# Masks, denominators and state of the Taylor attention put in another order on VectorE, and TensorE four score units behind instead of five

## The chip, the cores and the metric

One core of one Trainium2 chip runs the whole program. The metric is the time of one execution on the device in microseconds (us). The engines are TensorE (PE, with its weight loads PEld), VectorE (DVE), ScalarE (ACT), GpSimd (POOL) and SyncE (SP), which issues the DMAs. All five run their own instruction streams in order and meet at semaphores.

## The reference, cut to what matters

The input is 8 sequences of 1024 tokens of width 256. Each is layer-normed, and the output is the input plus two branches: a linear attention with a Taylor feature map (16 heads of width 16), which the change touches, and a two-layer transformer with local attention, which it does not.

```
xn = layernorm(x)                                     # (8, 1024, 256)
q, k, v = heads of xn @ Wq.T, xn @ Wk.T, xn @ Wv.T    # 16 heads of width 16
f(u)  = [1, u / 2, u_i * u_i / (4 * sqrt(2)), u_i * u_j / 4 for i < j]
y_t   = sum over s <= t of (f(q_t) . f(k_s)) * v_s  /  sum over s <= t of (f(q_t) . f(k_s))
out   = x + y @ Wo.T + transformer(xn)
```

The kernel uses that f(q) . f(k) is, up to a factor, (q.k + 4)^2 + 16. So a tile of scores is a matmul, a square with bias 4 on ACT, and a sum with 16; on a diagonal tile DVE also multiplies by the causal mask.

## The kernel before

The program does the Taylor attention for the 8 sequences first (0 to about 930 us), then the transformer. Within the first part, `project` and `attention` alternate: `project(b + 1, b)` makes q, k and v of the next sequence and finishes the output of the last one.

`attention(b)` goes over four groups of four heads, and each group over 14 score units (`UNITS`). Units 0 to 9 are the near tiles: five steps of two units each (a unit holds two heads). Unit 10 is the state: the first four key tiles, taken as 160 quadratic forms (`psi`, written by POOL's `pairs` and DVE's `other_rows`) times the values (`state`, L774). Units 11 and 12 are the forms applied to the late queries (L811), unit 13 the remaining forms (`rest`, L804).

- PE computes the scores of unit n (L816, L811, L804) into a ring of three bank pairs, so it first waits until unit n - 3 has been consumed. BEHIND units later it runs `attend` (L832, L839, L842), which multiplies the values with the squared and masked weights. With BEHIND = 5, `attend` of step 2 stands behind unit 10 and that of step 3 behind unit 12. After unit 11 stands `turn_state` (L782, L784), which transposes the state.
- ACT squares each unit (L663, L658 for unit 13) into `weights`. There are three sets of them, so the first unit of a step waits for `attend` of three steps before.
- DVE masks the diagonal tiles of each step (`mask_diagonals`, L452), copies the state out of PSUM (`keep_state`, L459), copies it back turned (`turn_state`, L466 and L467), adds the sums of earlier tiles to the result (`add_before`, L443, one for each half of the tokens), and prepares psi for the next group (`other_rows`, L480 to L490).
- The denominators of groups 0 to 2 go a longer way. After both L443 of a group, SP copies the denominator rows into a flat tile (L221), DVE inverts them (`invert_den`, L388), SP copies them back (L225), DVE spreads them over the partitions (`spread_den`, L393 and L395), and POOL multiplies (L320; after group 1 it also adds group 0, L323). Group 3 is normalised by DVE in eight pieces (`normalise`, L406 to L413), which wait for POOL's third L320.
- DVE also does other work in the groups: statistics of the next sequence (L367 in group 0, L372 and L375 in group 1), its layer norm (L382, four tiles in each of groups 2 and 3) and, in groups 1 and 3 of sequences 5 and 6, a scaling of tables (L537).
- SP's queue in a sequence is: `load_heads` of group 2 (12 DMAs, L254, once group 0's scores are all done), `invert` of group 0 (L221, then L225 once DVE has inverted), `load_heads` of group 3 (once group 1's scores are done), `invert` of group 1, `invert` of group 2, then the stores and loads for the next sequence.

In the names below, `shared` holds psi and the state, `t_ps` is PSUM, `qkT` are the transposed heads and `vals` the values.

Of the kernel before, what the change touches and what calls it, by code (L numbers as in the profile page):

```python
# [15 lines left out]
ALU = mybir.AluOpType  # L16
# [10 lines left out]
TH, TD = 16, 16  # L27
GROUPS, GH = 4, 4
# [9 lines left out]
ROW_PAIRS, ROW_SQUARES, ROW_LINEAR, ROW_ONE = 0, len(PAIRS_IJ), len(PAIRS_IJ) + TD, len(PAIRS_IJ) + 2 * TD  # L38
# [23 lines left out]
def taylor_block(nc, B, x, wqk, wv, wo, ident, causal, earlier, eps_rows, keep_rows, forms, own_head, later, xn_d, attn_d, parts_d, xnT_d,  # L62
                 id_s, ao, rot, qks_s, last_stored):

    with ExitStack() as ctx:
# [36 lines left out]
        psi = space[:, 0:PAST * GH * FORMS].rearrange("p (th f) -> p th f", f=FORMS)  # L102
# [93 lines left out]
        def unit_bank(n):  # L196
            return 2 + 2 * (n % RING)
# [163 lines left out]
        def _(dve):  # L361
            v = nc.vector

            def tile_stats(b, t):
                if t == 0:
                    dve.wait_ge(x_in, 16 * b + 16)
                v.bn_stats(st[:, t, :], xs[:, t, :]).then_inc(stats, 1)  # L367
# [9 lines left out]
            def layer_norm(b, t):  # L377
                if t == 0:
                    dve.wait_ge(rstd_ready, b + 1)
                    if b >= 1:  # L380
                        dve.wait_ge(stored, 16 * (2 * b - 1))
                v.tensor_scalar(xn[:, t, :], xs[:, t, :], mv[:, t, 0:1], rstd[:, t:t + 1],  # L382
                                ALU.subtract, ALU.mult).then_inc(xn_ready, 1)

            def invert_den(b, g):

                dve.wait_ge(den_in, 16 * (b * (GROUPS - 1) + g + 1))
                v.reciprocal(den_flat[:, :], den_flat[:, :]).then_inc(den_inverse, 1)  # L388

            def spread_den(b, g):  # L390

                dve.wait_ge(den_out, 16 * (b * (GROUPS - 1) + g + 1))
                v.stream_shuffle(den[:, :], den[:, :], [ONE[g % 2]] * 32).then_inc(spread, 1)  # L393
                dve.wait_ge(spread, 2 * (b * (GROUPS - 1) + g) + 1)
                v.tensor_scalar_mul(den[:, :], den[:, :], keep_s[:, g % 2:g % 2 + 1]).then_inc(spread, 1)  # L395
# [40 lines left out]
            def attention(b, following):  # L436
                def add_before(g, half):

                    tiles = slice(half * TILES // 2, (half + 1) * TILES // 2)
                    if g == 0 and half == 0:  # L440
                        dve.wait_ge(before_ready, b + 1)
                    dve.wait_ge(pv_done, (b * GROUPS + g) * AS + LAST_STEP[half] + 1)
                    v.tensor_tensor(yT[:, g, half * 512:(half + 1) * 512].rearrange("p (t n) -> p t n", n=P),  # L443
                                    ps[:, half, :].rearrange("p (t n) -> p t n", n=P),
                                    before[:, g, tiles].unsqueeze(2).to_broadcast([P, TILES // 2, P]), ALU.add).then_inc(yT_ready, 1)

                def mask_diagonals(g, i):
                    w = GH * ((g * AS + i) % RING)
                    dve.wait_ge(squared, (b * GROUPS + g) * SQUARES + 2 * i + 2)
                    for o, width in DIAGONALS[i]:  # L450
                        a = weights[:, w:w + GH, o:o + width]
                        last = v.scalar_tensor_tensor(a, a, 16.0, causal_s[:, 0:width].unsqueeze(1).to_broadcast([P, GH, width]),  # L452
                                                      ALU.add, ALU.mult)
                    last.then_inc(diag, 1)

                def keep_state(g):
                    group = b * GROUPS + g
                    dve.wait_ge(state_ps, group + 1)
                    v.tensor_copy(state_T, ps[:, unit_bank(g * NU + 2 * NS), 0:FORMS]).then_inc(state_kept, 1)  # L459

                def turn_state(g):
                    group, bank = b * GROUPS + g, unit_bank(g * NU + 2 * NS) + 1
                    dve.wait_ge(turned_ps, group + 1)
                    if group:
                        dve.wait_ge(pv_done, group * AS)
                    v.tensor_copy(state_main, ps[:, bank, 0:P])  # L466
                    v.tensor_tensor(state_rest, ps[:, bank, P:2 * P], own_s[:, 0:P], ALU.mult).then_inc(state_ready, 1)  # L467

                def other_rows(g):

                    group = b * GROUPS + g
                    if g == 0:
                        dve.wait_ge(krows_ready, PAST * (b + 1))
                        for half in parts_out:
                            dve.wait_ge(half, 16 * (BLOCKS // 2) * (b + 1))
                    if group:
                        dve.wait_ge(state_ps, group)
                    k = krows[:, g].rearrange("p t h d -> p (t h) d")
                    squares = psi[:, :, ROW_SQUARES:ROW_SQUARES + TD]
                    v.tensor_tensor(psi[:, :, ROW_LINEAR:ROW_LINEAR + TD], k, k, ALU.max)  # L480
                    v.reduce_sum(ksum[:, :], k, AX).then_inc(ksum_ready, 1)
                    dve.wait_ge(ksum_ready, 4 * group + 1)
                    v.tensor_scalar_add(ksum[:, :], ksum[:, :], 1.0).then_inc(ksum_ready, 1)
                    dve.wait_ge(ksum_ready, 4 * group + 2)
                    v.scalar_tensor_tensor(squares, k, 2.0, ksum[:, :].unsqueeze(2).to_broadcast([P, PAST * GH, TD]), ALU.mult, ALU.subtract)\
                        .then_inc(ksum_ready, 1)
                    v.tensor_scalar(psi[:, :, ROW_ONE:FORMS], ksum[:, :].unsqueeze(2).to_broadcast([P, PAST * GH, FORMS - ROW_ONE]),
                                    -1.0 / (FORMS - ROW_ONE), 3.0 / (FORMS - ROW_ONE), ALU.mult, ALU.add).then_inc(ksum_ready, 1)
                    dve.wait_ge(ksum_ready, 4 * group + 4)
                    v.tensor_tensor(squares, squares, k, ALU.mult).then_inc(psi_rest, 1)  # L490

                for g in range(GROUPS):
                    mask_diagonals(g, 0)
                    if g >= 1:
                        add_before(g - 1, 1)
                    if following is not None and g == 0:
                        for t in range(4):
                            tile_stats(following, t)
                    mask_diagonals(g, 1)
                    if g == 0:  # L500
                        other_rows(0)
                    if g >= 2:
                        spread_den(b, g - 2)
                    if following is not None:
                        if g == 0:
                            for t in range(4, TILES):
                                tile_stats(following, t)
                        if g == 1:
                            variances(following)
                        if g % 2 and b >= len(later):  # L510
                            scale_tables((b - len(later)) * 2 + g // 2)
                        if g >= 2:
                            for t in range(2):
                                layer_norm(following, (g - 2) * TILES // 2 + t)
                    mask_diagonals(g, 2)
                    if following is not None and g >= 2:
                        for t in range(2, 4):
                            layer_norm(following, (g - 2) * TILES // 2 + t)
                    mask_diagonals(g, 3)
                    keep_state(g)  # L520
                    mask_diagonals(g, 4)
                    turn_state(g)
                    add_before(g, 0)
                    if g + 1 < GROUPS:
                        other_rows(g + 1)
                    if g >= 1:
                        invert_den(b, g - 1)
                add_before(GROUPS - 1, 1)
                spread_den(b, GROUPS - 2)

            def scale_tables(quarter):

# [142 lines left out]
        def _(pe):  # L675
# [81 lines left out]
            def attention(b):  # L757
# [86 lines left out]
                    last.then_inc(pv_done, 1)  # L844

                units = GROUPS * NU
                BEHIND = 5
                last_of = {}
                for n in range(units):
                    kind, i, pair = UNITS[n % NU]  # L850
# [1 line left out]
                ends = {n: step for step, n in last_of.items()}  # L852
                for n in range(units + BEHIND):
                    if n < units:
                        scores(n)
                    if n - BEHIND in ends:
                        attend(*ends[n - BEHIND])
                    if n % NU == 2 * NS + 1 and n < units:
# [956 lines left out]
```

## Time and profile before

| what | us |
|---|---|
| median of three runs | 3529.01 |
| the three runs | 3529.01, 3528.80, 3537.74 |
| the profiled execution | 3529.01 |
| its span | 3527.10 |
| PE busy in the span | 3357.0 (95%) |
| DVE busy | 2763.9 (78%) |
| ACT busy | 2512.4 (71%) |
| POOL busy | 1575.1 (45%) |

The shares of the whole span mix two parts. In the last 2597 us the PE has next to no gap; in the first 930 us every engine has gaps, and the change is in that part only. So the times that matter are read inside one group of one sequence, from the timeline, and the part as a whole from the table of stretches.

### The profile page before, as it was taken

What the parts mean: (1) busy time and instruction counts of PE and PEld (TensorE: products, weight loads), DVE (VectorE), ACT (ScalarE), POOL (GpSimd) and SP (SyncE); (2) the same over time, 40 slices, a digit from 0 to 9 for tenths busy, and PEclk for the clock granted to TensorE, in tenths of its full rate; (3) what the DMA queues carried; (4) which work ended last, traced back from release to release, by engine and by line L of the source; (5) the groups of instructions that cost most, each with busy time, mean ns of one, the idle gap of its engine ahead of it and who ended that gap; (6) DMA issues with size and microseconds to landing.
All of it is one profiled execution on the core that took longest, in us unless ns stands there. A gap on an engine that the chain in (4) does not pass through costs nothing.

```text
span 3527.1 us, 96731 instructions
## 1 busy us (share of the span) xinstructions
PE 3357.0 (95%) x36960; PEld 2506.0 (71%) x36960; DVE 2763.9 (78%) x8288; ACT 2512.4 (71%) x5597; POOL 1575.1 (45%) x1675
## 2 busy tenths in 40 slices
PE   7888888889699999999999999999999999999999
PEld 4544554445378787887878878788787887878877
DVE  4767776776688888878888788887888888888886
ACT  5556665666377777777777777777777777777775
POOL 4445544454344444444444444444444444444443
PEclk9999999999899999999999999999999999999999
DMA  6646765567322222222222222222222222222211
GB/s 158 140 124 116 168 142 117 108 113 145 104 62 67 68 61 72 66 69 68 61 72 66 69 68 61 72 66 68 68 61 72 66 68 68 61 72 66 69 46 42
DMA packets 289965, 293.94 MB, mean 83 GB/s; under 512 B 40960, under 2 KB 221536, under 8 KB 288992
## 3 DMA queue, kind: packets, MB, share of 16 engines
q1 hardware_dynamic: 289504, 287.74, 34.0%
q8 instruction: 295, 4.83, 0.6%
q14 instruction: 166, 1.36, 0.1%
HBM read 104.89 MB, written 58.73 MB: 46 GB/s over the span
## 4 chain that ended last, share of the span: by engine, by line
PE 72%; DVE 1%; POOL 0%; ACT 0%; issue 0%; DMA 0%; SPq 0%; DVEq 0%; POOLq 0%
PE f_ps L1548 18%; PE f_ps L1656 16%; PE f_ps L1668 9%; PE f_ps L1633 6%; PE f_ps L1612 4%; PE f_ps L1553 3%; PE f_ps L1575 3%; PE f_ps L1593 3%; PE f_ps L1622 2%; PE f_ps L1582 2%; PE f_ps L1661 2%; PE f_ps L1597 2%; PE f_ps L1640 1%; PE f_ps L1534 0%; ACT pr L1464 0%
## 5 line engine op out<-in xcount | busy, mean ns | idle before, releaser
L1219 POOL TENSOR_TENSOR turned<-qk,rot 128x256 f32<-128x256 f32 x512 | 406.3, 814 | 1247.4 <-ACT qk L1431 1234.4
L1548 PE MATMUL f_ps<-wqkv_s,hT 128*128 128x512 f32 x1536 | 707.2, 596 | 9.2 <-DMA hT<-xnT_dram 5.7
L1656 PEld LDWEIGHTS f_ps<-hnT,w_s 128*128 128x128 f32 x5120 | 591.7, 192 | 62.9 <-issue 59.7
L1299 DVE CUSTOM_DVE_ANT_0 pr<-f_ps,masks_s 128x192 f32<-128x192 f32 x1024 | 326.5, 355 | 359.5 <-PE f_ps L1582 357.5
L1656 PE MATMUL f_ps<-hnT,w_s 128*128 128x128 f32 x5120 | 592.6, 275 | 2.5 <-DVE hnT L1356 2.5
L1464 ACT ACTIVATE pr<-pr,nmax,rnorm 128x192 f32<-128x192 f32 x1024 | 545.1, 535 | 43.4 <-DVE nmax L1306 43.4
L1548 PEld LDWEIGHTS f_ps<-wqkv_s,hT 128*128 128x128 f32 x1536 | 277.2, 191 | 273.4 <-issue 186.4
L1316 DVE TENSOR_SCALAR pr<-pr,rsum 128x192 f32<-128x192 f32 x1024 | 446.8, 498 | 9.0
L1668 PE MATMUL f_ps<-w_s,act_u 128*128 128x256 f32 x1536 | 352.8, 380 | 0.0
L663 ACT ACTIVATE weights<-t_ps,four_s 128x1024 f32<-128x1024 f32 x320 | 330.4, 1120 | 27.3 <-PE t_ps L842 12.5
L1226 POOL TENSOR_TENSOR rnorm<-ssq,f_mhalf 128x8 f32<-128x8 f32 x128 | 255.8, 1998 | 163.5 <-DVE ssq L1276 163.5
L1668 PEld LDWEIGHTS f_ps<-w_s,act_u 128*128 128x128 f32 x1536 | 282.2, 190 | 32.7
L1453 ACT ACTIVATE kT<-f_ps 128x512 f32<-128x512 f32 x128 | 76.4, 597 | 293.3 <-PE f_ps L1553 293.3
L337 POOL TENSOR_TENSOR shared<-krows 128x240 f32<-128x240 f32 (+14 forms) x480 | 251.5, 559 | 65.2 <-PE t_ps L774 33.2
L1488 ACT ACTIVATE act_u<-f_ps,b_s 128x128 f32<-128x128 f32 x640 | 205.1, 364 | 105.0 <-PE f_ps L1661 89.8
L1633 PE MATMUL f_ps<-fwo_s,oT 128*128 128x256 f32 x1024 | 242.5, 380 | 0.3 <-ACT oT L1477 0.3
L452 DVE SCALAR_TENSOR_TENSOR weights<-weights,causal_s 128x512 f32<-128x512 f32 (+1 forms) x192 | 185.5, 984 | 71.0 <-ACT weights L663 70.8
L832 PE MATMUL t_ps<-weights,vals 128*32 128x512 f32 (+3 forms) x2048 | 191.0, 478 | 38.7 <-DVE weights L452 35.7
L816 PE MATMUL t_ps<-qkT 96*32 96x128 bf16 (+3 forms) x4096 | 188.9, 305 | 31.2 <-ACT weights L663 19.3
L1266 DVE TENSOR_TENSOR cosine<-qk,rot 128x512 f32<-128x512 f32 x256 | 207.7, 811 | 11.8 <-ACT qk L1431 11.8
L1366 DVE SCALAR_TENSOR_TENSOR act_u<-f_ps,b_s,act_u 128x128 f32<-128x128 f32 (+1 forms) x768 | 208.3, 340 | 6.7 <-ACT act_u L1488 4.2
L1233 POOL TENSOR_TENSOR rnorm<-ssq,f_mhalf 128x8 f32<-128x8 f32 x128 | 208.9, 1632 | 0.0
(150 smaller groups left out, 6827.3 us busy)
## 6 DMA issues: line engine op xcount, KB each, us to landing
vw<-vw SPq DMA_DIRECT2D x628, 128.0 KB, 2.4
qkT<-parts_dram SPq DMA_DIRECT2D x384, 128.0 KB, 5.7
kT<-kT SPq DMA_DIRECT2D x124, 256.0 KB, 2.7
parts_dram<-shared SPq DMA_DIRECT2D x64, 384.0 KB, 2.6
xnT_dram<-xnT SPq DMA_DIRECT2D x8, 1025.0 KB, 4.7
xs<-x_dram SPq DMA_DIRECT2D x8, 1024.0 KB, 7.3
xn_dram<-xn SPq DMA_DIRECT2D x8, 1024.0 KB, 5.1
attn_dram<-ao SPq DMA_DIRECT2D x8, 1024.0 KB, 9.9
```

The costliest lines, as they stand in the source:

```text
L337: last = g.tensor_tensor(psi[:, :, o:o + width], k[:, :, i:i + 1].to_broadcast([P, PAST * GH, width]), k[:, :, i + 1:TD], ALU.mult)
L663: a.activation(weights[:, w:w + 2, :], ps[:, bank:bank + 2, :], ACT.Square, bias=four_s[:, :] if kind == "near" else zero_s[:, :]).then_in ...
L1219: g.tensor_tensor(turned[:, heads, f], qk[:, heads, z], sines, ALU.mult).then_inc(done, 1)
L1226: g.tensor_tensor(rnorm[:, HEADS:], ssq[:, HEADS:], mhalf[:, HEADS:], ALU.pow).then_inc(knorm_ready, 1)
L1233: g.tensor_tensor(rnorm[:, :HEADS], ssq[:, :HEADS], mhalf[:, :HEADS], ALU.pow).then_inc(qnorm_ready, 1)
L1299: last = v.tensor_tensor_reduce(out=chances(h), in0=ps[:, SCORES[p], k * 256:k * 256 + BAND], in1=mask_of(it)[:, HALF - k * HALF:HALF - k ...
L1316: last = v.tensor_scalar_mul(chances(h), chances(h), rsum[:, h:h + 1])
L1464: last = a.activation(chances(h), chances(h), ACT.Exp, bias=nmax[:, h:h + 1], scale=rnorm[:, h:h + 1], accum_out=psum[:, h:h + 1])
L1548: last = mm(ps[:, b, :], rows, wqkv_s[:, l, c, i * INNER:(i + 1) * INNER], start=(c == 0), stop=(c == KC - 1))
L1633: last = mm(ps[:, WO, 0:DIM], oT[:, c, :], wo_s[:, l, c, :], start=(c == 0), stop=(c == INNER // P - 1))
L1656: last = mm(ps[:, UP[j // 2], o:o + P], w1_s[:, l, c, half * FULL + j * P:half * FULL + j * P + P], hnT[:, c, :], start=(c == 0), stop=(c ...
L1668: last = mm(ps[:, DOWN, 0:DIM], act_u[:, j, :], w2_s[:, l, j, :], start=(j == 0), stop=(j == FB - 1))
```

## The change

Four edits, all in the Taylor attention:

1. `other_rows` copies k with `tensor_copy` instead of `tensor_tensor(k, k, max)` (L480).
2. DVE's order in a group changes. `add_before(g, 0)` now stands ahead of `keep_state(g)`, and both behind the mask of step 4. `invert_den(g - 1)` moves from the end of the group to behind the mask of step 2.
3. `spread_den(g - 1)` now stands between `keep_state(g)` and `turn_state(g)`; before, it stood one group later, behind the mask of step 1, and for group 2 at the end of the sequence.
4. BEHIND is 4 instead of 5. So `attend` of step 2 stands ahead of the state, and that of step 3 ahead of `turn_state`.

```
-                    v.tensor_tensor(psi[:, :, ROW_LINEAR:ROW_LINEAR + TD], k, k, ALU.max)
+                    v.tensor_copy(psi[:, :, ROW_LINEAR:ROW_LINEAR + TD], k)
...
                     mask_diagonals(g, 1)
                     if g == 0:
                         other_rows(0)
-                    if g >= 2:
-                        spread_den(b, g - 2)
...
                     mask_diagonals(g, 2)
+                    if g >= 1:
+                        invert_den(b, g - 1)
                     if following is not None and g >= 2:
                         for t in range(2, 4):
                             layer_norm(following, (g - 2) * TILES // 2 + t)
                     mask_diagonals(g, 3)
+                    mask_diagonals(g, 4)
+                    add_before(g, 0)
                     keep_state(g)
-                    mask_diagonals(g, 4)
+                    if g >= 1:
+                        spread_den(b, g - 1)
                     turn_state(g)
-                    add_before(g, 0)
                     if g + 1 < GROUPS:
                         other_rows(g + 1)
-                    if g >= 1:
-                        invert_den(b, g - 1)
                 add_before(GROUPS - 1, 1)
-                spread_den(b, GROUPS - 2)
...
-                BEHIND = 5
+                BEHIND = 4
```

On PE, around the state of a group, the row before is this (L774 state, L832 attend, L811 units 11 and 12, L782 and L784 the turn, L804 unit 13):

```order
L774 MATMUL t_ps<-shared,vals 32x160 x16
L832 MATMUL t_ps<-weights,vals 32x384 x4
L832 MATMUL t_ps<-weights,vals 32x128 x4
L811 MATMUL t_ps<-qkT,forms_s 32x512 x8
L782 MATMUL t_ps<-id_s,shared 32x128 x4
L784 MATMUL t_ps<-id_s,shared 32x128 x4
L811 MATMUL t_ps<-qkT,forms_s 32x512 x8
L832 MATMUL t_ps<-weights,vals 32x256 x8
L804 MATMUL t_ps<-qkT,forms_s 32x512 x4
L816 MATMUL t_ps<-qkT 32x512 x8
L832 MATMUL t_ps<-weights,vals 32x384 x4
L832 MATMUL t_ps<-weights,vals 32x128 x4
```

and after the change, where every line number from here on is one lower (L831 is attend, L810 are units 11 and 12, L815 the near scores):

```order
L831 MATMUL t_ps<-weights,vals 32x384 x4
L831 MATMUL t_ps<-weights,vals 32x128 x4
L773 MATMUL t_ps<-shared,vals 32x160 x16
L810 MATMUL t_ps<-qkT,forms_s 32x512 x8
L831 MATMUL t_ps<-weights,vals 32x256 x8
L781 MATMUL t_ps<-id_s,shared 32x128 x4
L783 MATMUL t_ps<-id_s,shared 32x128 x4
L810 MATMUL t_ps<-qkT,forms_s 32x512 x8
L803 MATMUL t_ps<-qkT,forms_s 32x512 x4
L831 MATMUL t_ps<-weights,vals 32x384 x4
L831 MATMUL t_ps<-weights,vals 32x128 x4
L815 MATMUL t_ps<-qkT 32x512 x32
```

Attend of step 2 (the first two rows) has passed the state, attend of step 3 (the 32x256 row) has passed the turn and unit 12, and attend of step 4 has passed the first scores of the next group.

On DVE, group 2 of a sequence from the mask of step 1 on stands like this before (L452 masks, L393 and L395 the spread, L382 layer norm, L459 keep, L466 and L467 turn, L443 add):

```order
L393 STREAM_SHUFFLE den<-den 128x1024
L395 TENSOR_SCALAR den<-den,keep_s 128x1024
L382 TENSOR_SCALAR xn<-xs,t_mv,t_rstd 128x256 x2
L452 SCALAR_TENSOR_TENSOR weights<-weights,causal_s 128x4x256
L382 TENSOR_SCALAR xn<-xs,t_mv,t_rstd 128x256 x2
L452 SCALAR_TENSOR_TENSOR weights<-weights,causal_s 128x4x128 x2
L459 COPY shared<-t_ps 128x160
L452 SCALAR_TENSOR_TENSOR weights<-weights,causal_s 128x4x256
L466 COPY shared<-t_ps 128x128
L467 TENSOR_TENSOR shared<-t_ps,own_s 128x128
L443 TENSOR_TENSOR yT<-t_ps,before 128x512
```

and like this after it:

```order
L382 TENSOR_SCALAR xn<-xs,t_mv,t_rstd 128x256 x2
L452 SCALAR_TENSOR_TENSOR weights<-weights,causal_s 128x4x256
L388 RECIPROCAL den_flat<-den_flat 128x32
L382 TENSOR_SCALAR xn<-xs,t_mv,t_rstd 128x256 x2
L452 SCALAR_TENSOR_TENSOR weights<-weights,causal_s 128x4x128 x2
L452 SCALAR_TENSOR_TENSOR weights<-weights,causal_s 128x4x256
L443 TENSOR_TENSOR yT<-t_ps,before 128x512
L459 COPY shared<-t_ps 128x160
L393 STREAM_SHUFFLE den<-den 128x1024
L395 TENSOR_SCALAR den<-den,keep_s 128x1024
L466 COPY shared<-t_ps 128x128
```

The copy of the state (L459) has gone behind the last mask and behind L443, which waits for attend of step 3; the reciprocal stands ahead of the mask of step 3; the spread stands inside the turn.

## Rows read from the trace of the kernel before

**Rows 1.** Stretches: busy time of each engine, clock share, DMA share, GB/s.

```profile
0.00:930.00 930.00, 781.70 (x9952) 441.43 (x9952) 653.54 (x1248) 576.41 (x866) 429.91 (x632) 0.94 0.59 127
930.00:3527.00 2597.00, 2575.31 (x27008) 2064.53 (x27008) 2110.35 (x7040) 1935.99 (x4731) 1145.22 (x1044) 1.00 0.26 68
```

**Rows 2.** Timeline, sequence 3, group 0: start, us, engine, line, idle before and releaser.

```profile
391.62 10.15 ACT L663 ACTIVATE weights<-t_ps,four_s 128x1024 f32<-128x1024 f32 x10 [0.18 <-PE t_ps L816]
...
400.52 2.79 DVE L452 SCALAR_TENSOR_TENSOR weights<-weights,causal_s 128x1024 f32<-128x1024 f32 x3
...
401.87 1.07 PE L832 MATMUL t_ps<-weights,vals 128*32 128x384 f32 x16
...
402.73 0.64 PE L811 MATMUL t_ps<-qkT,forms_s 96*32 96x512 bf16 x8
...
403.24 0.31 DVE L459 COPY shared<-t_ps 128x160 f32<-128x160 f32 x1
...
404.73 1.11 ACT L663 ACTIVATE weights<-t_ps,zero_s 128x1024 f32<-128x1024 f32 x1 [0.20 <-PE t_ps L811]
...
405.69 0.69 DVE L443 TENSOR_TENSOR yT<-t_ps,before 128x512 f32<-128x512 f32 x1 [0.47 <-PE t_ps L832]
```

**Rows 3.** Timeline, sequence 3, group 1, SP, ACT and PE.

```profile
405.80 6.63 SPq L254 DMA_DIRECT2D qkT<-parts_dram  x12
...
406.40 1.11 ACT L663 ACTIVATE weights<-t_ps,four_s 128x1024 f32<-128x1024 f32 x1
...
415.52 1.29 PE L774 MATMUL t_ps<-shared,vals 128*32 128x160 f32 x32
416.63 1.05 PE L832 MATMUL t_ps<-weights,vals 128*32 128x384 f32 x16
```

**Rows 4.** Timeline, sequence 3, group 2.

```profile
420.74 4.24 ACT L663 ACTIVATE weights<-t_ps,four_s 128x1024 f32<-128x1024 f32 x4
...
424.17 6.96 SPq L254 DMA_DIRECT2D qkT<-parts_dram  x12
...
426.64 1.34 DVE L393 STREAM_SHUFFLE den<-den 128x1024 f32<-128x1024 f32 x1
...
428.69 2.78 DVE L382 TENSOR_SCALAR xn<-xs,t_mv,t_rstd 128x256 f32<-128x256 f32 x2
428.85 2.47 POOL L320 TENSOR_TENSOR yT<-yT,den 128x1024 f32<-128x1024 f32 x1 [4.31 <-DVE den L395]
...
431.17 0.56 SPq L221 DMA_DIRECT2D den_flat<-yT  x1
...
432.92 1.21 DVE L382 TENSOR_SCALAR xn<-xs,t_mv,t_rstd 128x256 f32<-128x256 f32 x2
...
434.04 1.90 DVE L452 SCALAR_TENSOR_TENSOR weights<-weights,causal_s 128x512 f32<-128x512 f32 x2
...
440.59 1.11 ACT L663 ACTIVATE weights<-t_ps,four_s 128x1024 f32<-128x1024 f32 x1
```

**Rows 5.** DMA packets from 435 to 437 us (den_flat's are the 128-byte ones).

```profile
DMA packets 215, 0.15 MB, mean 77 GB/s; under 512 B 155, under 2 KB 155, under 8 KB 214
```

**Rows 6.** Timeline, end of sequence 3: last attend, next sequence's transposes, DVE's chain.

```profile
462.10 1.04 PE L842 MATMUL t_ps<-shared 128*32 128x512 f32 x8
...
463.07 0.66 PE L685 MATMUL t_ps<-id_s,xn 128*128 128x128 f32 x4
...
475.00 0.69 DVE L419 TENSOR_TENSOR rest<-t_ps,shared 128x512 f32<-128x512 f32 x1 [0.68 <-ACT shared L595]
```

**Rows 7.** Timeline, end of sequence 7, the last.

```profile
905.73 0.69 DVE L443 TENSOR_TENSOR yT<-t_ps,before 128x512 f32<-128x512 f32 x1 [2.79 <-PE t_ps L842]
...
911.32 0.30 DVE L406 STREAM_SHUFFLE den<-yT 128x128 f32<-128x128 f32 x1 [0.36 <-issue]
```

**Rows 8.** Groups of instructions by line, DVE, first 930 us.

```profile
L480 DVE TENSOR_TENSOR shared<-krows 128x256 f32<-128x256 f32 x32 | 17.9, 559 | 0.0
```

**Rows 9.** Stretch 457 to 460 us, columns as in rows 1.

```profile
457.00:460.00 3.00, 3.00 (x40) 1.60 (x36) 1.25 (x3) 1.11 (x1) 0.00 (x0) 0.51 0.00 0
```

## The prediction

> **What bounds the kernel now.** I first read the table of stretches [rows 1]. In the last 2597 us PE is busy 2575 of them and the change does not reach it; all that can move lies in the first 930 us, where PE is busy 782, DVE 654, ACT 576 and POOL 430. No engine is full there, so waits inside a group decide, and the next view is the timeline of one group. I take sequence 3 and count from a group's first square on ACT. The reader should see that ACT's ten near squares run without a gap in group 0 (10.15 us for ten, one each 1.0 us, [rows 2]), and that every gap comes after them, where ACT waits for units 11 and 12. Groups 0 and 1 last 14.8 (391.62 to 406.40) and 14.3 us (406.40 to 420.74); groups 2 and 3 have the layer norm and the spread on DVE, and group 2 lasts 19.85 (420.74 to 440.59) [rows 2 to 4]. From group 3's first square to PE's first transpose of the next sequence it is 463.07 - 440.59 = 22.5 us [rows 4, 6]. From there on PE, ACT and DVE go hand in hand to the next sequence. DVE is not the late one: its first subtraction there (L419) still waits 0.68 us for ACT [rows 6].
>
> **Group 0: what the new order costs.** Before, `keep_state` (L459) ran at 403.24, as soon as the mask of step 3 was done, and unit 12 was squared at 404.73, that is 13.1 us into the group [rows 2]. In the change L459 stands behind the mask of step 4 and behind L443, and L443 waits for attend of step 3, which itself has the state and unit 11 ahead of it on PE. Step by step, from the group's start: the mask of step 2 begins at 8.9 (the three L452 begin at 400.52), attend of step 2 can start at 10.2, as now (401.87). Before, the state was already done by then; now it comes behind. Attend takes 0.86 (401.87 to 402.73 on PE), the state 1.11 (415.52 to 416.63 [rows 3]), unit 11 0.44 (an estimate from the 0.64 of its row less the overlap): attend of step 3 starts at 12.65. L443 can read 1.2 later, 13.85 (its wait ends 405.69, with attend of 16 matmuls begun just before), takes 0.69, and L459 0.31: 14.8. PE's turn takes 0.44 and unit 12 ends 0.66 after its start, so its square begins at 15.9 instead of 13.1. Square 13 follows at 16.9. The next group's first score now stands behind attend of step 4 as well: rest scores at 16.05, attend 16.25 to 17.1, the score 0.6, so the next group starts at 17.75. Group 0: **+3.0 us**. The masks and squares themselves hide nothing of it, because ACT has nothing else to square: all three rings are full.
>
> **Group 1.** Here there is a gain first: attend of step 5 stands one unit earlier, so ACT's fifth square starts at 4.0 instead of 4.8. The mask of step 2 can be done at 7.4 (square 5 done at 6.1, the mask 1.2). Then DVE reaches the moved reciprocal (L388), and this adds a wait: it needs the denominators, which SP fetches (L221) only behind the 12 DMAs of `load_heads`. Their first is issued when the last group's scores are done, 0.6 before the group's start now (405.80) and, by the steps above, 1.3 before it then. In group 2 the 12 go out from 424.17, L221 at 431.17, and 155 of its packets under 512 bytes (it has 128; a few tiny ones are others) are only seen from 435 to 437 [rows 4, 5]: about 12.3 us from the first of the 12 to the last byte. With that distance the reciprocal runs at 11.0 - 0.3 = 10.7 in group 1, which I take; the bounds are 7.4 (no wait at all, if the small DMA came at its own pace) and 12. Queued behind it on DVE are the masks of steps 3 and 4, and PE's attend of step 3 waits for the first of them. Masks of step 3 beside POOL's pairs take 1.90 (434.04 [rows 4]): done 12.9; attend of step 3; mask of step 4 to 14.1; L443 to 14.75; L459 15.05; then the spread (L393 and L395, from 426.64 to 428.69, 2.05) to 17.1, beside which PE's turn and unit 12 are hidden; turn on DVE 0.5 to 17.6; rest scores, attend, first score, 0.2 + 0.86 + 0.66: 19.4 against 14.3, **+5.1 us**. Without the wait it would be 17.1, +2.8.
>
> **Group 2.** The spread and POOL's multiply are gone from ahead of the mask of step 2. That was worth 2.05, and 1.57 more, since the first pair of L382 took 2.78 beside POOL's L320 and the second 1.21 [rows 4]. So the mask of step 2 is done at 7.5 instead of 12.2. But the reciprocal again waits, to 10.9 (12.3 from 1.4 before the start). Then: reciprocal 0.34, L382 pair 1.2, masks 1.9, mask 1.2, L443 and L459 1.0, spread 2.05, turn 0.5, and 1.7 for PE as before: 20.6 against 19.85, **+0.7 us**. Without the wait 18.4, -1.4.
>
> **Group 3 and the end.** No loads stand ahead of L221 here, so no wait. POOL's L320 and L323 now run around the group's start and hold the first two masks to about 6.2. From there: L382 pair, mask, reciprocal, pair, masks, mask come to 12.6, L443 and L459 to 13.6, spread 15.7, turn 16.2, rest scores 16.5, the two last attends 0.86 and 1.8 to 19.2. That is 22.5 - 19.2 = **-3.3 us**. In sequences 0 to 6 nothing more comes of DVE's freed 2.05 and of the POOL multiply at the end (DVE waits for ACT there). Only in sequence 7 do they sit in the open: from the end of the last L443 (906.42) to the first L406 (911.32) are 4.9 us [rows 7], of which some 4.5 go, with a group 3 shorter by some 3: -7. Its group 2 has no layer norm in either kernel, so it gains less: +2.
>
> **The clock.** PE's granted clock was 0.51 from 457 to 460 us [rows 9], its 1.2 GHz level, after PE had stood waiting for L459. It now waits so, 1 to 2.5 us at a time, in all four groups, not in two. What stands in the open behind the wait is rest scores, attend, first score: 1.7 us at 2.4 GHz, so up to 1.7 more per group, nothing at the least. I take 0.5 each, nearer to nothing since groups 0 and 1 run with shorter gaps: +2.0 per sequence.
>
> **Copy for max (L480).** 559 ns each, 32 times, 17.9 us in all [rows 8]. DVE then waits for squares 0 and 1 of the next group anyway, and that hides it: nothing. The bounds are -0.3 and +2.5 us each in the group's wait, the latter if it is caught behind an L320.
>
> **Two rules of the Trainium skill.** In the trace the denominators' packets came after the twelve loads' [rows 4, 5]. The Trainium skill, DMA: Bandwidth & Descriptors, section Queues, rings and completion order, says that on each DMA engine descriptors of a ring are consumed in ring order, and that engines alternate only between rows; L221 and the loads are both SP's. By that rule the wait on L388 is sure; the trace agrees, and the sum above has it.
> L382 beside L320 took 2.78 for a pair instead of 1.21. The Trainium skill, SBUF — State Buffer, section Who interferes with whom, says that DVE and GpSimd share a port pair as a lock held for the whole instruction, and names copies and instructions with two SBUF inputs among those that take it. By that rule the loser waits for up to a whole L320, and the new L480 is no safer than the old one; the price of it is the third rival.
>
> **Sum.** Sequences 0 to 6: 3.0 + 5.1 + 0.7 - 3.3 + 2.0 = +7.5 each, 52.5 together. Sequence 7: 3.0 + 5.1 + 2 - 7 + 2 = +5, of which I take 3, as its gaps are uneven. Together +55.5. On the profiled execution's 3529.01 (span 3527.10 and 1.9 around it), which is also the median, that gives **3584 us**.
>
> **Rivals.**
> 1. The denominators land in time. For it: in group 1 the loads need not be as slow as in group 2, whose 12.3 I measured. Against: both move the same amount. Groups 1 and 2 then come to +2.8 and -1.4, a sequence to +3.1 with the clock and +1.1 without: 3529 + 22 + 1 = 3552, or 3536 without the clock's part.
> 2. Faster: DVE's own work is the path in groups 2 and 3, so the 3.6 us (2.05 + 1.57) taken from ahead of the mask of step 2 arrive whole in both, and the chain L443, L459, turn hides beside it. It decides if the denominators are there by 7.4 us and if the two groups give back more than the 3.0 + 2.8 that groups 0 and 1 lose: -7.2 + 5.8 = -1.4, seven times, and -7 at the end: 3512. Against it: L459 has four things more ahead of it than before.
> 3. POOL's multiplies fall on the masks of groups 2 and 3 whole: 2.5 each (L320 took 2.47), of which I have some 0.4 in group 2 and part in group 3. About +4 a sequence: 3529 + 55 + 28 = 3612. Against: they start while DVE does `other_rows`.
> 4. The half clock in all four groups whole: 4 x 1.7 - 2.0 = 4.8 more each: about 3620.
>
> **How the numbers follow.** A difference within 0.3% (10.6 us) is one that a measurement cannot tell from none. The forecast has 0.60, rival 1 0.15, rival 2 0.10, rivals 3 and 4 together 0.15. Faster: rival 2 but for its nearest part, and a little for unseen gains, 0.10. Same: the low half of rival 1, 0.07. Slower 0.83. The range runs from the low part of rival 1, 3541, to 3608, short of rivals 3 and 4; the forecast's own is 3565 to 3600.
>
> **What would show it.** In the changed profile: PE's wait for L459 in all four groups and ACT's wait for units 11 and 12 (L810 there) well above before; a DVE wait of 2 to 4 us for a DMA at the reciprocal in groups 1 and 2, and none in group 3; groups 0 and 1 at 17 to 20 us; L382 pairs of 1.2 us; group 3 shorter; nothing changed after the Taylor part. If the reciprocal does not wait, group 1 is near 17 and rival 1 holds. If groups 0 and 1 stay under 16, the chain through L443 is wrong, and with it the sign.

## The result, and the profile after

The changed kernel takes 3592.11 us (median of four runs, 3582.77 to 3600.04) against 3532.41 for the kernel before (four runs): a ratio of 1.0167, 95% interval [1.0131, 1.0203]. A second comparison of almost the same kernel (the change with the old max, below) gave 1.0168 [1.0154, 1.0182]. The forecast was 3584. The profiled execution took 3588.62, its span is 3586.8.

The table of stretches, cut where the Taylor part ends, answers to [rows 1]: stretch, busy time of PE, PEld, DVE, ACT and POOL, clock share, DMA share, GB/s.

```profile
0.00:987.00 987.00, 802.98 (x9952) 441.29 (x9952) 629.84 (x1248) 575.09 (x866) 397.49 (x631) 0.92 0.56 119
987.00:3586.00 2599.00, 2578.08 (x27008) 2064.50 (x27008) 2110.58 (x7040) 1936.11 (x4731) 1145.54 (x1045) 1.00 0.26 68
```

The second part is as long as before (2599 to 2597 us). The first is 57 us longer. ACT and DVE do no more work in it than before, and PE is busy for 21 us more with the same matmuls, at a lower mean clock share: most of the 57 us is waiting. The waits of the first part name where (who waited for whom, us, times, longest). First the kernel before, in its 930 us:

```profile
ACT weights L663 <- PE t_ps L811: 114.4, 53, 7.6
PE t_ps L832 <- DVE weights L452: 35.7, 15, 5.4
```

and the changed kernel, in its 987 us:

```profile
ACT weights L662 <- PE t_ps L810: 164.4, 52, 8.1
PE t_ps L831 <- DVE weights L452: 60.8, 23, 4.3
DVE den_flat L388 <- DMA den_flat<-yT: 57.7, 16, 4.9
```

Two waits have grown, and the last line has no counterpart before: the reciprocal waits 16 times, 3.6 us each on average, in groups 1 and 2 of the eight sequences. Sequence 3 shows both costs. First group 0, which answers to [rows 2] (start, us, engine, line, idle before and its releaser):

```profile
409.02 10.15 ACT L662 ACTIVATE weights<-t_ps,four_s 128x1024 f32<-128x1024 f32 x10 [0.18 <-PE t_ps L815]
...
419.08 1.07 PE L831 MATMUL t_ps<-weights,vals 128*32 128x384 f32 x16 [2.24 <-DVE weights L452]
419.94 1.98 PE L773 MATMUL t_ps<-shared,vals 128*32 128x160 f32 x32
...
424.34 0.69 DVE L443 TENSOR_TENSOR yT<-t_ps,before 128x512 f32<-128x512 f32 x1 [3.07 <-PE t_ps L831]
424.94 0.32 DVE L459 COPY shared<-t_ps 128x160 f32<-128x160 f32 x1
425.31 0.43 PE L781 MATMUL t_ps<-id_s,shared 128*32 128x128 f32 x8 [1.10 <-DVE shared L459]
...
426.44 1.11 ACT L662 ACTIVATE weights<-t_ps,zero_s 128x1024 f32<-128x1024 f32 x1 [2.51 <-PE t_ps L810]
```

The near squares still run without a gap, and attend of step 2 starts 10.1 us into the group, as forecast (10.2). Then come the state, unit 11, attend of step 3, L443 and L459 one behind the other: L459 starts 15.9 us into the group (11.6 before) and unit 12's square 17.4 us (13.1 before). Each is about 1.5 us later than the working had them (about 14.5, and 15.9). The state took 1.98 us, not 1.29 as in [rows 3]: PE had waited 2.24 us, and from 419 to 424 us its granted clock was 0.66, so it was at the lower level (1.2 GHz) for most of that time.

Group 1, against [rows 3]:

```profile
428.32 10.15 ACT L662 ACTIVATE weights<-t_ps,four_s 128x1024 f32<-128x1024 f32 x10 [0.20 <-PE t_ps L815]
...
433.42 0.57 SPq L221 DMA_DIRECT2D den_flat<-yT  x1
...
440.63 0.35 DVE L388 RECIPROCAL den_flat<-den_flat 128x32 f32<-128x32 f32 x1 [4.92 <-DMA den_flat<-yT]
440.90 3.05 DVE L452 SCALAR_TENSOR_TENSOR weights<-weights,causal_s 128x512 f32<-128x512 f32 x3
...
442.73 1.94 PE L831 MATMUL t_ps<-weights,vals 128*32 128x256 f32 x16 [4.18 <-DVE weights L452]
...
447.68 1.11 ACT L662 ACTIVATE weights<-t_ps,zero_s 128x1024 f32<-128x1024 f32 x1 [7.96 <-PE t_ps L810]
447.77 2.35 POOL L320 TENSOR_TENSOR yT<-yT,den 128x1024 f32<-128x1024 f32 x1 [2.12 <-DVE den L395]
...
448.00 2.27 DVE L480 COPY shared<-krows 128x256 f32<-128x256 f32 x1
```

The reader should follow one wait through three engines: DVE stands 4.92 us for the denominators, so the mask of step 3 is late, PE stands 4.18 us for it with attend of step 3, and ACT stands 7.96 us ahead of unit 12. The wait also costs PE its clock. The stretches of group 1, in the kernel before and in the changed one (columns as above), have a clock share of 1.00 and 0.78:

```profile
406.40:420.70 14.30, 13.73 (x284) 7.88 (x280) 10.81 (x27) 12.92 (x14) 9.19 (x17) 1.00 0.65 129
428.00:451.00 23.00, 16.93 (x284) 7.98 (x276) 13.85 (x29) 13.20 (x14) 11.40 (x17) 0.78 0.54 82
```

Group 2 repeats the wait, 2.78 us long. There the pair of L382 no longer meets L320 [rows 4]:

```profile
456.12 0.73 DVE L382 TENSOR_SCALAR xn<-xs,t_mv,t_rstd 128x256 f32<-128x256 f32 x2
...
461.51 0.35 DVE L388 RECIPROCAL den_flat<-den_flat 128x32 f32<-128x32 f32 x1 [2.78 <-DMA den_flat<-yT]
...
473.46 4.12 ACT L662 ACTIVATE weights<-t_ps,four_s 128x1024 f32<-128x1024 f32 x4 [1.87 <-PE t_ps L815]
```

Sequence 3 is not a mean one: it lost 12.6 us, the most of all; the others lost 2.8 to 8.2. Taken from ACT's squares in sequences 0 to 6, the mean time from a group's first square to the next group's is (group 3's includes the projection behind it):

| us | group 0 | group 1 | group 2 | group 3 | sum |
|---|---|---|---|---|---|
| before | 15.2 | 15.4 | 19.8 | 61.9 | 112.3 |
| after | 18.4 | 22.2 | 21.7 | 57.5 | 119.9 |
| difference | +3.2 | +6.8 | +1.9 | -4.4 | +7.6 |
| forecast, with 0.5 for the clock | +3.5 | +5.6 | +1.2 | -2.8 | +7.5 |

### The profile page after: what moved, and what is told of

Its sections match the earlier page's. It is cut to its first block, busy times and chain, and to the rows that moved or that the text cites. A ratio compares the mean times of both kernels' runs of the same rounds, so it can differ in the third digit from the quotient of the medians.

```text
span 3586.8 us, 96731 instructions
## 1 busy us (share of the span) xinstructions
PE 3381.1 (94%) x36960; PEld 2505.8 (70%) x36960; DVE 2740.4 (76%) x8288; ACT 2511.2 (70%) x5597; POOL 1543.0 (43%) x1675
## 4 chain that ended last, share of the span: by engine, by line
PE 71%; DVE 1%; ACT 0%; issue 0%; POOL 0%; DMA 0%; SPq 0%; DVEq 0%; POOLq 0%
PE f_ps L1547 18%; PE f_ps L1655 16%; PE f_ps L1667 9%; PE f_ps L1632 6%; PE f_ps L1611 4%; PE f_ps L1552 3%; PE f_ps L1574 3%; PE f_ps L1592 3%; PE f_ps L1621 2%; PE f_ps L1581 2%; PE f_ps L1660 2%; PE f_ps L1596 2%; PE f_ps L1639 1%; PE f_ps L1533 0%; ACT pr L1463 0%; DVE pr L1298 0%
## 5 line engine op out<-in xcount | busy, mean ns | idle before, releaser
L337 POOL TENSOR_TENSOR shared<-krows 128x240 f32<-128x240 f32 (+14 forms) x480 | 227.4, 510 | 187.8 <-PE t_ps L773 157.0
L452 DVE SCALAR_TENSOR_TENSOR weights<-weights,causal_s 128x512 f32<-128x512 f32 (+1 forms) x192 | 176.8, 946 | 105.0 <-ACT weights L662 104.8
L831 PE MATMUL t_ps<-weights,vals 128*32 128x512 f32 (+3 forms) x2048 | 193.2, 490 | 64.6 <-DVE weights L452 60.8
L1282 DVE TENSOR_TENSOR qk<-cosine,turned 128x512 f32<-128x512 f32 x256 | 206.8, 808 | 0.0
```

The costliest lines, as they stand in the source:

```text
L337: last = g.tensor_tensor(psi[:, :, o:o + width], k[:, :, i:i + 1].to_broadcast([P, PAST * GH, width]), k[:, :, i + 1:TD], ALU.mult)
```

## The experiments

All ratios are to the kernel before. Each experiment's group times are means as in the table above.

**BEHIND alone.** The kernel before with

```
-                BEHIND = 5
+                BEHIND = 4
```

> The kernel before with BEHIND = 4 alone; DVE's order, the denominators and the max as before. Theory: TensorE's order is only part of the cost. In group 0 attend of steps 2 and 3 now stand ahead of the state and the turn, unit 12's square comes at about 14.6 instead of 13.1, the group lasts 16.5 to 17 us (15.2 before, 18.4 in the change); group 1 about 14.5, groups 2 and 3 within 1 us of before. In all +15 to +25 us over the kernel before (about 3550). Rival: BEHIND alone is the cost: +45 us or more, group 0 at 18 us. Second rival: one unit less behind frees ACT's rings sooner and nothing else happens: -5 to -15 us.

Measured: 3525.6 us, 0.9976 [0.9965, 0.9986]. My theory had the direction in group 0 right and its size too small (17.7, +2.6, where I had 16.5 to 17), and it had the sum wrong: 10 us less instead of 15 to 25 more. Groups 2 and 3 gave back 1.8 and 1.6 us. The number is that of the second rival, but not its mechanism, since group 0 does lose. In groups 2 and 3 the masks are late: in sequence 3, group 2 of the kernel before, PE stood 1.59 us for L459 with attend of step 3 still behind the turn; here that attend runs ahead of the turn, and PE does not stand there. So this part of the change, by itself, is a small gain and not a part of the loss.

**The copy alone**, the first edit of the change.

> The kernel before with the tensor_copy of L480 alone. Theory: the copy takes less than the 559 ns of the max, but DVE waits for squares right after it: no change (within 3 us). Rival: the copy is held by whole GpSimd instructions and delays masks: +5 us or more, with single copies of 1 us and longer.

Measured: 3535.9, 1.0004 [0.9990, 1.0018]. No change.

**The keep back in its place**, in the changed kernel:

```
                     mask_diagonals(g, 3)
+                    keep_state(g)
                     mask_diagonals(g, 4)
                     add_before(g, 0)
-                    keep_state(g)
```

> The changed kernel with keep_state back ahead of the mask of step 4 (add_before(g, 0) stays ahead of spread and turn). Theory: the chain L443, L459, turn is what group 0 loses, so group 0 goes from 18.4 to about 16.5 us; in groups 1 to 3 unit 12 is squared 2 to 3 us sooner, but VectorE's turn still stands behind L443 and the spread and ends the group, so these change by less than 1 us. In all -15 to -25 us against the changed kernel (about 3570). Rival: the late keep costs in every group: -50 us or more. Second rival: keep's place is indifferent: within 5 us.

Measured: 3568.0, 1.0100 [1.0078, 1.0123], 24 us below the change. Group 0 went from 18.4 to 17.35, with unit 12 squared at 14.6 us instead of 15.9 (medians of sequences 0 to 6), and groups 1 to 3 changed by 0.7 us or less. The sum is as expected. Group 0, which I had at 16.5, is not, and in groups 1 to 3 unit 12's square came only 0.8 to 1.5 us sooner (means), where I had 2 to 3.

**The denominators' DMA from ScalarE**, in the changed kernel; L221 leaves SP's `invert`:

```
+                    if n % NU == 6 and n > NU:
+                        ...
+                        act.dma_start(den_flat[:, :], yT[ONE[g % 2]:P:VP, g, :]).then_inc(den_in, 16)
                     act.wait_ge(score_ps, b * GROUPS * SQUARES + squares_to(n) + 1)
```

> The changed kernel with the first denominator DMA (L221) issued by ScalarE ahead of its square of unit 6 instead of by SyncE behind the 12 loads. Theory: the reciprocal's wait comes from the place in SyncE's queue, so the DMA lands some 2 to 3 us after its issue, the reciprocal runs at about 8 to 9.5 us in groups 1 and 2 (12.3 and 10.2 in the change), group 1 goes from 22.2 to 17.5-19 us and group 2 from 21.7 to 19-20; in all -30 to -55 us against the changed kernel. Rival: the bytes of the loads keep the 16 engines busy and the small DMA waits for them whoever issues it: reciprocal as late as before, within 5 us of the changed kernel.

Measured: 3584.0, 1.0140 [1.0120, 1.0159]; its interval overlaps that of the change. The theory fell: I had 30 to 55 us less. The timeline of its sequence 3, group 1:

```profile
433.14 0.56 ACTq L654 DMA_DIRECT2D den_flat<-yT  x1
...
440.44 0.35 DVE L386 RECIPROCAL den_flat<-den_flat 128x32 f32<-128x32 f32 x1 [4.39 <-DMA den_flat<-yT]
```

From issue to use it is 7.3 us, as from SP (433.42 to 440.63: 7.2). The DMA is issued 4.5 us into the group here and 5.1 in the changed kernel, because it waits for L443 in both. So the run changes its queue and hardly the time of its issue. The DMA queues from 436 to 438 us (packets, MB, share), where q10 is ACT's and q1 SP's:

```profile
q1 hardware_dynamic: 172, 0.28, 106.2%
q10 hardware_dynamic: 39, 0.00, 3.5%
```

From 433 to 436 us the view shows packets of q1 alone; q10's first came 4.5 us after the issue. So a queue of its own did not bring the small DMA forward while the loads kept the engines full.

**The loads made small.** The changed kernel, where the 12 loads for groups 2 and 3 bring 128 of 1024 columns; the rest of these groups' heads is left out.

```
-                        sp.dma_start(qkT[g % 2][i * TD:(i + 1) * TD, a, :, :],
+                        n = SEQ if g < 2 else P
+                        sp.dma_start(qkT[g % 2][i * TD:(i + 1) * TD, a, :, 0:n],
```

> The changed kernel, but the 12 loads for groups 2 and 3 of each sequence bring only the first 128 of 1024 columns; the rest of these groups' heads is left out, so its output is not the reference's, and all counts and waits stay. Theory (the last run points to it: the denominators' DMA was late even when ScalarE issued it): it is the bytes of the loads, 1.5 MB at some 140 GB/s, that hold the denominators back; without them the reciprocal runs at 7.5 to 9 us in groups 1 and 2, group 1 lasts 17 to 18.5, group 2 18.5 to 19.5, and the kernel loses -40 to -60 us against the changed one. Rival: the number of DMAs and their place ahead of it count: reciprocal above 10 us, under 15 us gained.

Measured: 3522.8, 0.9965 [0.9951, 0.9978], 69 us below the change. The median start of the reciprocal went from 11.8 and 10.5 us into groups 1 and 2 to 7.3 and 7.4, group 1 from 22.2 to 18.2 and group 2 from 21.7 to 17.5. Sequence 3, group 2:

```profile
429.65 0.56 SPq L221 DMA_DIRECT2D den_flat<-yT  x1
...
432.63 0.35 DVE L389 RECIPROCAL den_flat<-den_flat 128x32 f32<-128x32 f32 x1
```

The number of DMAs ahead of the denominators and their queue are the same here, and only the bytes are fewer. So it is the bytes of the loads that hold the denominators.

**The denominators where they were**, in the changed kernel: `invert_den` at the group's end, `spread_den` one group later, as in the kernel before.

> The changed kernel with the denominators where they were: invert_den at the end of a group, spread_den one group later. Kept are BEHIND 4, the copy, and L443 ahead of keep_state. Theory: the wait of the reciprocal goes, so group 1 comes to 16 to 17 us (22.2), group 2 to 20 to 21, but the multiply stands beside the layer norm again and group 3 with the projection behind it gets longer by 3 (57.5 to about 60.5), group 0 stays at 18.4: in all -20 to -35 us against the changed kernel, still +20 or more above the kernel before. Rival: L443 ahead of keep costs nothing once the reciprocal does not wait: as fast as BEHIND 4 alone (3526).

Measured: 3559.6, 1.0068 [1.0051, 1.0085], 32 us below the change. The sum is as expected. Groups 18.3, 16.2, 19.6 and 61.6: group 2 is a little under my 20 to 21, and group 3 with the projection over my 60.5. Against BEHIND alone (3525.6) this kernel differs by L443 and the mask of step 4 ahead of the keep and by the copy, and is 34 us slower: that is the chain through L443.

**Denominators in the gaps.** The kernel before, with the denominators' steps moved and nothing else (their old places, not shown, are empty):

```
                     keep_state(g)
+                    if g >= 1:
+                        invert_den(b, g - 1)
                     mask_diagonals(g, 4)
                     turn_state(g)
+                    if g >= 1:
+                        spread_den(b, g - 1)
                     add_before(g, 0)
```

> The kernel before (BEHIND 5, max) with its masks, keep, turn and L443 as they were, and the denominators earlier: invert_den(g - 1) behind keep_state, spread_den(g - 1) between turn_state and add_before(g, 0), where VectorE waited 1.9 us for TensorE in group 2. Theory: the mask of step 2 in groups 2 and 3 comes 2 to 3.6 us sooner, nothing is put in its place, and the end of a sequence is shorter: -30 to -45 us against the kernel before. Rival: the reciprocal meets the loads' bytes here too (group 1: it is due at 11, they end at 12) and GpSimd's multiply falls on the masks: within 10 us of before.

Measured: 3477.6, 0.9838 [0.9817, 0.9859]: 56 us faster, more than the 30 to 45 I had expected. Groups 15.5, 16.1, 16.0 and 58.7. The reciprocal still waits for its DMA in groups 1 and 2: 12 times of 16, 18.9 us in all and 2.7 at the longest.

**The other gaps.** As the last, but

```
                     mask_diagonals(g, 0)
+                    if g >= 2:
+                        spread_den(b, g - 2)
...
                     turn_state(g)
+                    if g >= 1:
+                        invert_den(b, g - 1)
                     add_before(g, 0)
...
+                spread_den(b, GROUPS - 2)
                 add_before(GROUPS - 1, 1)
```

> As the last, but invert_den(g - 1) behind turn_state (due at 13 us or later, when the loads have ended in any case) and spread_den(g - 1) in the next group behind the mask of step 0, where VectorE waits for TensorE's attend of step 5. Theory: as fast as the last within 5 us; faster if there the reciprocal waited, slower if the multiply now meets the layer norm again. Both come 20 us or more below before. Rival: as before.

Measured: 3468.4, 0.9809 [0.9790, 0.9828], and once more with more runs:

> The kernel of e8 once more, on the chip of this comparison, to have its gain with more runs. It should be 1.7 to 2.1% faster than the kernel before.

Measured: 3471.1, 0.9813 [0.9797, 0.9829]. This is the fastest of all, 64 us below the kernel before, and 9 us below the last one. I had the two within 5 us, unless the reciprocal waited in the last one, which it did. Groups 15.3, 15.5, 15.4 and 58.3. In sequence 3, group 2:

```profile
398.23 1.35 DVE L393 STREAM_SHUFFLE den<-den 128x1024 f32<-128x1024 f32 x1
...
400.44 2.37 POOL L320 TENSOR_TENSOR yT<-yT,den 128x1024 f32<-128x1024 f32 x1 [1.64 <-DVE den L395]
400.88 2.48 DVE L452 SCALAR_TENSOR_TENSOR weights<-weights,causal_s 128x512 f32<-128x512 f32 x1
...
409.70 0.34 DVE L388 RECIPROCAL den_flat<-den_flat 128x32 f32<-128x32 f32 x1
```

The reciprocal is due when the loads have ended, and waits for nothing; that is what the last kernel still lacked. Something is left: the mask of step 1 takes 2.48 us beside L320 instead of 0.68.

**The same with BEHIND = 4.**

> The last kernel (denominators in VectorE's gaps) with BEHIND = 4. Theory: BEHIND 4 gained 0.24% alone because in groups 2 and 3 the late mask of step 2 was what TensorE waited for, and the state no longer waited behind it; with that mask early, what is left of it is group 0's loss of 2.5 us, partly paid back by attend of step 5 standing earlier: +5 to +20 us against the last kernel (3468). Rival: its gain adds up: -8 us.

Measured: 3512.7, 0.9944 [0.9932, 0.9957]: 44 us slower than with 5, more than twice what I had expected. Groups 18.4, 16.4, 17.4 and 59.1. In group 0 the state has gone behind attend of step 2, and with it out of PE's idle time. PE, here and then in the kernel with BEHIND = 5:

```profile
398.46 1.07 PE L832 MATMUL t_ps<-weights,vals 128*32 128x384 f32 x16 [2.47 <-ACT weights L663]
399.32 2.32 PE L774 MATMUL t_ps<-shared,vals 128*32 128x160 f32 x32
```

```profile
374.02 1.29 PE L774 MATMUL t_ps<-shared,vals 128*32 128x160 f32 x32 [0.18 <-ACT weights L663]
...
376.01 1.07 PE L832 MATMUL t_ps<-weights,vals 128*32 128x384 f32 x16 [0.69 <-ACT weights L663]
```

The state takes 2.32 us instead of 1.29. The granted clock of the 3 us around it is 0.57 with BEHIND = 4 (most of them at the lower level, 1.2 GHz) and 1.00 with 5 (all at 2.4 GHz). That is group 0; the 1 to 2 us in groups 1 and 2 I did not take apart.

**L443 ahead of the keep, with the denominators in the gaps** (BEHIND 4, the max):

```
-                    keep_state(g)
                     mask_diagonals(g, 4)
+                    add_before(g, 0)
+                    keep_state(g)
                     turn_state(g)
                     if g >= 1:
                         invert_den(b, g - 1)
-                    add_before(g, 0)
```

> As e9, with add_before(g, 0) ahead of keep_state and both behind the mask of step 4, as in the change; the denominators stay in the gaps, the max stays. Theory: this measures the chain attend of step 3, L443, L459, turn by itself, without the wait of the reciprocal: 1 to 1.5 us in each of 32 groups, +30 to +45 us against e9 (group 0 near 18.3, groups 1 and 2 near 16.5 to 17). Rival: without the denominators' wait the chain is hidden: within 10 us of e9.

Measured: 3544.0, 1.0030 [1.0018, 1.0042], 31 us slower than the same without it. As expected in sum, though nothing of it is in group 0 (18.3 in both, where attend of step 3 came late either way), 0.7 to 0.8 in groups 1 and 2, and 1.7 in group 3 with the projection. So the chain is worth 31 to 34 us in two settings: here, and in the kernel with the denominators where they were.

**The change with the max.**

> The changed kernel with the max (tensor_tensor) back at L480. In the changed kernel copies at the end of groups 1 and 2 take 2.27 us beside GpSimd's L320. Theory: the max has two inputs and is held as well, and VectorE waits for squares behind it in any case: within 5 us of the changed kernel (3591). Rival: only the copy is held, and its 2 us in two groups of each sequence reach the next group's start: -15 to -30 us against the changed kernel.

Measured: 3595.9, 1.0168 [1.0154, 1.0182]. The longest max takes 2.55 us, the longest copy of the changed kernel 2.27: both are held.

## Why the prediction was right

*Group 0, +3.0.* Measured +3.2. The step that attend of step 3, L443 and L459 would stand in a row ahead of unit 12 is what the rows show, and two runs that take the chain away price it at 31 to 34 us of the whole. The working had the state behind attend of step 2 among its terms, but called the whole loss that of the late keep. Putting the keep back brought group 0 only from 18.4 to 17.35, and BEHIND 4, by which the state stands behind attend of step 2, had 17.7 by itself. So in group 0 the first cause is BEHIND 4.

*Group 1, +5.1.* Measured +6.8. The wait was the one forecast and longer: the reciprocal ran at 11.8 us (median) where I took 10.7. The loads were not slower. From the issue of the first of the twelve to the last byte of the denominators it was 12.2 us on average, and I had 12.3. But the working set the reciprocal 0.3 us ahead of that byte, for which no row stands, and it ran 0.9 us behind it. The rest goes with the clock: in sequence 3 attend of step 3 took 1.94 us, against 1.05 in group 0 before. With small loads, that is without the wait, the group came to +2.8, as I had said.

*Group 2, +0.7.* Measured +1.9. The reciprocal came at 10.5, near the 10.9 I took, but by two errors that cancel: it ran behind the last byte as in group 1, and the loads went out 2.6 us ahead of the group's start, not 1.4, since that start was itself late. The terms of the working add up to 20.8 and not to the 20.6 it gives. Attend of step 3 took 2.06 us here. With small loads the group came to -2.4, where I had -1.4.

*Group 3 with the end, -3.3.* Measured -4.4, and the reciprocal waits for nothing there. From the group's first square to PE's first transpose it is 19.0 us on average, where the working had 19.2. What it had wrong is the time before: it took the 22.5 of sequence 3, and the mean is 23.3.

*The sum.* By the medians the change costs 59.7 us, and the forecast had 55. In a mean sequence the forecast of +7.5 and the measured +7.6 are closer than their parts, which are off by -0.3, +1.2, +0.7 and -1.6. And sequence 3, on which it was worked out, changed by +4.5, +8.7, +2.3 and -2.8, together +12.6. That one sequence's working met the mean of seven that run from +2.8 to +12.6 is luck in part. No luck is what held in every part: the sign of each group, a wait for the denominators in groups 1 and 2 and none in group 3, and next to nothing in the second part of the program.

*The reason for the wait* was wrong in part. I had said that SP fetches the denominators only behind its 12 loads, which it does, and that the trace agreed with the Trainium skill, DMA: Bandwidth & Descriptors, section Queues, rings and completion order, on rings served in order. The trace could not tell queue from bytes. ScalarE's queue did not help (7.3 us from issue to use), smaller loads did. The same section says that engines alternate between rows at every packet; here, while q1 was full, q10's first packet came 4.5 us after the DMA's issue, and 1.2 us after it in group 3, where no loads stand ahead.

*POOL's multiply.* By rival 3 it would fall on masks. It fell on `other_rows` (L480 2.27 us), which hid it, since DVE then waits for squares in any case. The port lock that the Trainium skill, SBUF — State Buffer, section Who interferes with whom, describes would hold copy and max alike, and it did.

*The copy.* Nothing, as said: 1.0004 alone.

*The clock.* I had taken +0.5 us in each group. The granted clock of the two profiles, summed over sequences 0 to 6, has PE at its lower level for 1.4, 0.4, 5.4 and 6.5 us of a mean group 0, 1, 2 and 3 before (group 3 up to the next sequence's first transpose), and for 2.1, 8.2, 7.2 and 2.8 after. So nearly all of the new slow time is in group 1, where it is 2.9 us with the small loads, that is without the wait; and group 3 has less than before: there the 0.5 had the wrong sign. What these microseconds cost no row gives by itself.

*The last sequence.* +4.2 us by the same squares (groups 0 to 2 +11.4, the end -7.2); I had +3, with -7 for the end. The 53 us of the other seven and this make the 57.

*The balance of the parts*, by ratio: BEHIND 4 alone -0.2%; L443 ahead of the keep +0.9% on top; the denominators' new places +1.0% on top, which is a wait worth 2.0% (the small loads) less a gain of 1.0%. These shares hold in this order only: with the denominators in the gaps BEHIND 4 costs 1.3%. Nor can the new order of DVE be tried with BEHIND = 5. Attend of step 3 would then stand behind the turn, the turn waits for L459, and L459 stands behind L443, which waits for that attend: none of the three could start. The rival that had the denominators land in time, 3552 or 3536, was itself too high: with small loads it is 3522.8. And the faster rival had its mechanism right in part: the 3.6 us ahead of the mask of step 2 do arrive, if the reciprocal doesn't wait and the keep isn't held back, as the gaps' kernel shows.

## What to carry to other kernels

When a step that needs a DMA's result moves forward in an in-order engine, ask what else the 16 DMA engines carry at that moment: in sequence 3 a DMA of 16 KB took 7.2 us from issue to use beside 1.5 MB of loads, whichever queue they were on, and 3 us where the loads were an eighth of that. Put a short step of an engine where that engine waits in any case (here 64 us, from two moves), and don't put one that waits for a matmul's result ahead of one that the same matmul engine waits for (here 31 to 34 us).

## What the runs showed of the hardware that I had not expected

- A 16 KB DMA issued by ScalarE on a queue of its own (q10) had its first packet 4.5 us after its issue at 433.14, while SP's queue held the 16 engines (106% from 436 to 438 us). Over the groups 1 and 2 of all sequences it was 2.8 to 5.6 us, and in group 3, without loads, 1.2.
- Here a DMA's bytes had landed some 0.9 us before the engine that waited for them went on: the reciprocal ran 0.8 to 1.1 us after the last packet of the denominators in group 1 of the changed kernel.
- A small DVE instruction can be held as long as a large one: L483, 128x16, took 1.94 us beside POOL's L323, against 0.17 in the group before. In the changed kernel, sequence 3, end of group 2:

```profile
472.29 2.35 POOL L323 TENSOR_TENSOR yT<-yT 128x1024 f32<-128x1024 f32 x1
...
472.73 1.94 DVE L483 TENSOR_SCALAR ksum<-ksum 128x16 f32<-128x16 f32 x1
```

- Work put into PE's idle time can itself be cheaper: the state took 1.29 us at a granted clock of 1.00 in it, and 2.32 at 0.57 behind a wait of 2.47 us.
